# LSTM recurrence: the tanh of the cell goes to PSUM instead of SBUF

## The reference, cut to what matters

```python
def step(carry, xp):            # 6250 times, one after the other
    h, c = carry
    gates = xp + h @ W_hh.T     # xp: the projection of x, all of it made before
    i, f, g, o = jnp.split(gates, 4, axis=-1)
    c = jax.nn.sigmoid(f) * c + jax.nn.sigmoid(i) * jnp.tanh(g)
    h = jax.nn.sigmoid(o) * jnp.tanh(c)
    return ((h, c), h)
```

## Time and profile before

| what | value |
| --- | --- |
| median of three timed runs | 15332.19 us |
| lowest and highest of them | 15328.35 and 15332.62 us |
| span of the profiled execution | 15328.1 us |
| busy in that span: PE, PEld, DVE, ACT, POOL | 12930.1, 11447.9, 6928.1, 6961.0, 2775.5 us |
| stretch of the recurrence | about 4732 to 15212 us of the span |

### The profile page before, as it was taken

One profiled execution on the slowest core, in us unless ns is written; L12 is line 12 of the kernel. 1 busy time (PEld: TensorE's weight loads), 2 busy tenths in 40 slices (PEclk: granted clock), 3 DMA queues, 4 the chain that ended last, 5 costly groups with the idle time before them and its releaser, 6 DMA issues. The chain is left out here.

```text
span 15328.1 us, 1969280 instructions
## 1 busy us (share of the span) xinstructions
PE 12930.1 (84%) x904808; PEld 11447.9 (75%) x904808; DVE 6928.1 (45%) x45649; ACT 6961.0 (45%) x42309; POOL 2775.5 (18%) x4500
## 2 busy tenths in 40 slices
PE   3677586775858999999999999999999999999998
PEld 2466465664747888888888888888888888888886
DVE  4655656656553333333333333333333333333335
ACT  2354453543623444444444444444444444444443
POOL 4372672745720000000000000000000000000000
PEclk7889788897979999999999999999999999999998
DMA  3242451433431000000000000000000000000000
GB/s 78 75 148 68 123 159 52 141 94 101 152 102 39 2 2 2 2 2 2 2 2 2 2 2 2 2 2 2 2 2 2 2 2 2 2 2 2 2 2 18
DMA packets 673162, 542.61 MB, mean 35 GB/s; under 512 B 537743, under 2 KB 588953, under 8 KB 660764
## 3 DMA queue, kind: packets, MB, share of 16 engines
q1 hardware_dynamic: 450480, 316.45, 7.2%
q0 software_dynamic: 221600, 223.50, 6.0%
q10 hardware_dynamic: 934, 0.99, 0.0%
HBM read 286.52 MB, written 252.14 MB: 35 GB/s over the span
## 5 line engine op out<-in xcount | busy, mean ns | idle before, releaser
L1433 PE MATMUL p_g<-ring,wh 128*32 128x16 f32 x800000 | 8205.0, 186 | 699.3 <-DVE ring L1532 612.4
L1433 PEld LDWEIGHTS p_g<-ring,wh 128*32 128x32 f32 x800000 | 7592.7, 109 | 1474.3 <-DVE ring L1532 1155.0
L1474 ACT ACTIVATE cell<-p_g 128x3 f32<-128x3 f32 x12500 | 2180.2, 174 | 5556.8 <-PE p_g L1433 5556.8
L1526 DVE CUSTOM_DVE_ANT_1 cj<-cell 128x4 f32<-128x4 f32 x12500 | 2035.9, 163 | 5666.5 <-ACT cell L1474 5666.5
L1477 ACT ACTIVATE tc<-cell 128x1 f32<-128x1 f32 x12500 | 2482.2, 199 | 0.0
L1567 POOL COPY hist<-ring 128x6 f32 x2501 | 471.4, 188 | 10381.6 <-POOLq L1566 10381.6
L1532 DVE SCALAR_TENSOR_TENSOR ring<-og,tc 128x1 f32<-128x1 f32 x12500 | 1995.8, 160 | 776.7 <-ACT tc L1477 2.4
L411 POOL DMA_INDIRECT eb<-node_tab,eidx x1650 | 2060.8, 1249 | 622.5 <-issue 447.3
L1479 ACT ACTIVATE og<-p_g 128x1 f32<-128x1 f32 x12500 | 2042.4, 169 | 2.5 <-PE p_g L1433 2.3
L1407 PE MATMUL p_g<-xq,idn 128*32 128x24 f32 (+3 forms) x80032 | 1614.5, 189 | 61.7 <-PEq L1420 15.9
L1407 PEld LDWEIGHTS p_g<-xq,idn 128*32 128x32 f32 x80032 | 1254.3, 110 | 231.7 <-issue 16.0
(11 more groups left out here) (221 smaller groups left out, 7291.0 us busy)
## 6 DMA issues: line engine op xcount, KB each, us to landing
edge_tab<-eb SPq DMA_DIRECT2D x96, 1391.1 KB
edge_tab<-eb SPq DMA_DIRECT2D x96, 758.8 KB
eb<-node_tab,eidx POOLq DMA_INDIRECT x1650, 5.5
xp_tab<-xo SPq DMA_DIRECT2D x50, 500.0 KB, 2.6
xq<-xp_tab SPq DMA_DIRECT2D x1251, 8.0 KB, 1.7
xq<-xp_tab SPq DMA_DIRECT2D x1250, 12.0 KB, 1.7
x<-w_in SPq DMA_DIRECT2D x8, 1024.0 KB
out<-ot SPq DMA_DIRECT2D x25, 250.0 KB
```

The costliest lines, as they stand in the source:

```text
L1433: m = pe.matmul(to[32 * q:32 * q + 32], wh[:, k, D * q + 32 * c:D * q + 32 * c + 32], ring[:, (s - 1) % TS, k:k + 1].broadcast_to([128, w] ...
L1474: act.activation(cell[:, s, k, 0:6:2], gate_at(h, u, k)[:, :, 0], ACT.Tanh).then_inc(l_s[k], 1)
L1526: dve.tensor_tensor_reduce(cj[:, k, :].rearrange("p (a b) -> p a b", a=2), cell[:, s, k, 0:4].rearrange("p (a b) -> p a b", a=2), cell[:, ...
```

## The change

ACT writes the tanh of the cell to one column of a PSUM bank and DVE reads it there. For half k of a step the bank is `p_g[h][2 * k]`, that is `p_g[h][0]` for half 0 and `p_g[h][2]` for half 1, and the column is 508 + u, where u is the step's place in its bank (0, 1 or 2). Neither the gates nor the inputs nor the filling matmuls use these columns. `tc` shrinks to two columns, which serve only the first ACT operation ahead of the loop. No instruction, wait or semaphore is added, removed or moved on any engine.

```diff
-                og, tc = sb(sub, "og", [128, 2, KC]), sb(sub, "tc", [128, 2, KC])
+                og, tc = sb(sub, "og", [128, 2, KC]), sb(sub, "tc", [128, 2])
...
+                def tanh_at(h, u, k):
+
+                    return p_g[h][2 * k][:, 508 + u:509 + u]
...
-                    act.activation(tc[:, 0, :], tc[:, 1, :], ACT.Tanh)
+                    act.activation(tc[:, 0:1], tc[:, 1:2], ACT.Tanh)
...
                             def tanh_c(k):
-                                return act.activation(tc[:, (s % 2), k:k + 1], cell[:, (s + 1) % TS, k, 5:6], ACT.Tanh)
+                                return act.activation(tanh_at(h, u, k), cell[:, (s + 1) % TS, k, 5:6], ACT.Tanh)
...
                             def new_h(k):
-                                dve.scalar_tensor_tensor(ring[:, s, k:k + 1], og[:, (s % 2), k:k + 1], 1.0, tc[:, (s % 2), k:k + 1],
+                                dve.scalar_tensor_tensor(ring[:, s, k:k + 1], og[:, (s % 2), k:k + 1], 1.0, tanh_at(h, u, k),
                                                          ALU.add, ALU.mult).then_inc(l_h[turn((s + 1) % TS)[0]][k], 1)
```

## The result

Four timed runs of the changed kernel have a median of 15198.34 us (15195.38 to 15205.47); the kernel before, timed in the same job, has 15330.27 us. The ratio is 0.9915, with a 95% interval of 0.9903 to 0.9927: faster by 132 us. That is inside the range and 53 us above the predicted 15145 us.

What follows compares the result with a forecast made beforehand. A state-to-state chain closed by half 1, 1.677 us a step, was the bound. Saving 30 ns on the write and 0 on the read over 6250 steps gives 188 us, hence 15145 us; 8-in-10 range 15095 to 15335 us.

Steps and rivals of the forecast that it cites:

- The path of half 1, closed without slack: Chain from PE's second load burst through half 1's gates, second tanh and `new_h(1)` sets the step, 1.677 us.
- The write, -30 ns: ACT's second tanh of the cell, writing PSUM instead of SBUF, gets 30 ns shorter per step.
- The step from ACT's read to ACT's write: ACT's tanh reads PSUM 30 ns quicker than SBUF (169 against 199 ns); the same 30 ns was assumed for writing.
- The read, 0: DVE's `new_h` reading the tanh from PSUM instead of SBUF costs nothing, staying at 160 ns.
- That path then has 0.01 us left, so half 1 still decides and the saving stands in full: Half 0's path, 0.04 us from deciding, keeps 0.01 us after the 30 ns saving; all 188 us stand.
- half 0 takes over: Rival, chance 0.20: write savings beyond about 35 ns are lost as half 0 closes the step; about 15113 us.
- One sign: PE's second load burst should start about 0.26 us behind the first instead of 0.29, with steps of about 1.645 us.

Runs made afterwards that it cites:

- half0_only: Changed kernel, but only half 0's tanh of the cell goes to PSUM and half 1's stays in SBUF: 15329.67 us, 1.0002 of the kernel before.
- og0_before: Kernel before the change, with half 0's o gate written to a free column of a PSUM bank: 15332.99 us, ratio 1.0002.
- half1_only: Changed kernel, but only half 1's tanh of the cell goes to PSUM and half 0's stays in SBUF: 15218.27 us, 0.9930 of the kernel before.
- half1_late_before: Kernel before the change, with PE multiplying a half 1 of the state one step older, waiting for the new one only before the o gates: 15227.92 us, ratio 0.9929.
- w8_after: Changed kernel with 8 instead of 16 equal columns in each matmul of the state: 15263.80 us, 0.9947 of the kernel before.

## Why the prediction was right, and which term was off

- **The path of half 1, closed without slack:** right for the kernel before. `half0_only` and `og0_before` change nothing, while `half1_only` and `half1_late_before` both shorten the step.
- **The write, -30 ns:** right, 29 ns on the path (mean 199 to 172 over both halves). The step from ACT's read to ACT's write held here. As a rule it would mislead: it doesn't add up when the other end is in PSUM already (163 against 168 ns).
- **The read, 0:** slightly too careful; 160 to 155 ns. The wide rows, with 0 to 16 ns in favour of PSUM, told more than the rule in the Trainium skill ("Perfetto Trace Analysis", section "Optimizing Scalar/DVE Operations"), by which the read would have cost 65 ns more. The measurement decides: at one column, DVE's row is 5 ns shorter out of PSUM. The other rule of the Trainium skill, that ScalarE writes PSUM sooner than SBUF ("ScalarE: Activation LUTs", section "Step-by-step: what each stage is for"), agrees, with 27 ns.
- **"That path then has 0.01 us left, so half 1 still decides and the saving stands in full":** the term that was mis-sized. I gave half 0 a slack of about 0.035 us; it had 16.4 ns (`half1_late_before`), and 4.6 more come from `new_h(0)` reading PSUM: 21.0 ns, the measured gain. So the rival "half 0 takes over" is what happened, at 21 ns and not at 35. Its mechanism was named; its price, and with it the choice between it and the forecast, was wrong. That the time lay in the range was in part luck: a saving of 34 ns was cut to 21 by the path that the forecast took to stay clear. One sign is met and yet misleads: the second burst of loads does begin 0.26 us behind the first, with the 0.01 us left that the sum gave the loads, but the step is 1.654 us and not 1.645.

Why the slack was mis-sized can be read from the starts of single matmuls (medians over some 5900 steps, counted from the end of `new_h(0)`). I took the stop from the weight loads, the next of which came about 0.04 us after it was due. But loads run ahead of their matmuls, by 30 ns at the 33rd where nothing stops them (`half1_late_before`). The first matmul of the second burst came at 339 ns before and at 329 after: only 10 ns of the stop reached this matmul. The 56th, with which the first gates are nearly complete, came at 543 and then 526 ns, 17 ns sooner, and ACT's first gates at 794 and 777 ns. The rest of the loads' stop had been covered. From there the path of half 0 also leads through the gates of half 1, for ACT keeps its order: its second gates came at 1153 and 1136 ns, 17 ns sooner again, and in both kernels the first tanh of the cell starts 69 ns behind them and the o gate 93 ns behind that, whether that tanh takes 194 or 169 ns. In the coarser rows the same stands as 0.75 us from PE's start to ACT's first gates before (10002.44 to 10003.19) and 0.73 us after.

## What to carry to other kernels

When two paths close a loop, the slack of the second caps every gain on the first, and it has to be read where the consumer feels it (here at the gates that ACT reads), not at the stop of a prefetch that runs ahead. A quick way to know the cap is to take the leading path out of the race in one run and look at the step that is left: that run would have given 16 ns at once. And with operands of one column, the memory at each end is a fixed price worth measuring by pairs of rows: here PSUM was the cheaper end for ACT's write and, by a few ns, for DVE's read.

## What the runs showed of the hardware

ACT's tanh of one column took 194 to 203 ns from SBUF to SBUF, 168 to 171 ns from PSUM to SBUF, 169 to 174 ns from SBUF to PSUM, and 163 ns from PSUM to PSUM. By the same operation with its target moved, the first end in PSUM is worth 25 and 29 ns (the tanh of the cell of half 0 and of half 1), the second 5 ns (the o gate of half 0). DVE's `new_h` took 160 ns with both operands in SBUF, 158 ns with the o gate in PSUM and 155 ns with the tanh there. The granted clock fell to its lower level ahead of the recurrence, while PE stood idle for 15.9 us in the changed kernel and 15.7 us in `w8_after`; with half the columns in its matmuls it stayed there for about 0.5 ms, while with 16 columns the changed kernel had a mean of 0.96 in the first 168 us of the same stretch and 1.00 from there.
